# Decay attention: decays and inverse denominators kept as tokens by heads, and turned to heads by tokens

## What is computed

```
x_n   = layernorm(x) * ln1_w + ln1_b
q,k,v = x_n @ q_w + q_b, x_n @ k_w + k_b, x_n @ v_w + v_b        # (T, 128), 16 heads of 8
phi_q = elu(q) + 1 ;  phi_k = elu(k) + 1
lam   = maximum(sigmoid(x_n @ dec_w + dec_b), LAM_MIN)           # (T, 16): one decay per token and head
v_ext = concat([v, 1])                                           # nine columns per head
forward  S_t = S_(t-1) * lam_t + phi_k_t * v_t                   # scan over the tokens
backward R_t = lam_t * (phi_k_t * v_t + R_(t+1))                 # scan from the last token back
out   = phi_q . (S + R)                                          # summed over a head's 8 features
attn  = out[..., :8] / maximum(out[..., 8:], EPS)
x     = x + attn @ o_w + o_b
```

## Time and profile before

| what | us |
|---|---|
| median of 3 runs (lowest, highest) | 1849.06 (1844.62, 1851.38) |
| the profiled execution | 1840.17 |
| its span, first to last instruction | 1838.4 |
| first block of decay attention | 1371 to 1428 |
| second block of decay attention | 1428 to 1592 |

### The profile page before, as it was taken

How to read it: one execution, slowest core, us unless ns; L and a number is a source line. 1 busy time by engine, 2 the same in 40 slices (tenths; PEclk the granted TensorE clock), 3 DMA queues, 4 the chain that set the end, 5 groups by cost and what they waited for, 6 DMA issues and landing times. The chain is left out here.

```text
span 1838.4 us, 21584 instructions
## 1 busy us (share of the span) xinstructions
PE 1607.5 (87%) x7285; PEld 675.5 (37%) x7285; DVE 1352.3 (74%) x1951; ACT 856.2 (47%) x1493; POOL 222.4 (12%) x145
## 2 busy tenths in 40 slices
PE   6987589999999999999998799899984446589999
PEld 3433212222222222222223344466651112266665
DVE  5775798888888888888851777556666999745554
ACT  2443417777777777777776434322223000132221
POOL 2222300000000000000000122211100334201110
PEclk8998659999999999999999999899996767799999
DMA  6000310011001100120000000000000000000000
GB/s 171 4 0 1 124 30 8 15 28 37 12 15 28 33 15 15 28 32 10 2 2 1 1 0 0 1 1 0 0 1 0 0 1 0 1 1 6 6 6 7
DMA packets 32017, 29.42 MB, mean 16 GB/s; under 512 B 7789, under 2 KB 27033, under 8 KB 31929
## 3 DMA queue, kind: packets, MB, share of 16 engines
q1 hardware_dynamic: 31928, 28.31, 6.1%
HBM read 22.13 MB, written 4.19 MB: 14 GB/s over the span
## 5 line engine op out<-in xcount | busy, mean ns | idle before, releaser
L1350 DVE TENSOR_REDUCE mx<-ps 128x1 f32<-128x1024 f32 x512 | 603.1, 1219 | 108.9 <-PE ps L1262 107.6
L1338 ACT ACTIVATE xT<-ps 128x512 f32<-128x512 f32 x512 | 277.8, 598 | 123.4 <-PE ps L1285 117.0
L1262 PE MATMUL ps<-k,q 72*128 72x512 bf16 x1024 | 324.0, 399 | 11.0 <-DVE mx L1350 9.3
L1285 PE MATMUL ps<-q,k 84*128 84x512 bf16 x1024 | 311.7, 383 | 8.9 <-ACT xT L1338 6.4
L1338 ACT ACTIVATE xn<-ps 128x512 f32<-128x512 f32 x512 | 278.1, 601 | 83.9 <-PE ps L1285 79.1
L1285 PEld LDWEIGHTS ps<-q,k 84*128 84x128 bf16 x1024 | 96.4, 97 | 372.7 <-ACT xn L1338 152.6
L854 ACT ACTIVATE silu<-ps 128x512 f32<-128x512 f32 x144 | 85.3, 596 | 265.2 <-PE ps L827 261.8
L889 DVE TENSOR_TENSOR hid<-ps,silu 128x512 f32<-128x512 f32 x144 | 97.8, 689 | 90.2 <-PE ps L831 88.5
L827 PE MATMUL ps<-xT,ew 128*128 (+1 forms) x288 | 150.4, 604 | 6.4 <-PEq L1718 4.8
L817 PEld LDWEIGHTS ps<-ew,hid 128*128 128x128 f32 x1152 | 138.7, 192 | 30.6 <-issue 29.9
L831 PE MATMUL ps<-xT,ew 128*128 (+1 forms) x288 | 148.8, 599 | 0.0
(11 more groups left out here) (239 smaller groups left out, 1686.2 us busy)
## 6 DMA issues: line engine op xcount, KB each, us to landing
k<-k_parts SPq DMA_DIRECT2D x90, 64.0 KB
q<-q_parts SPq DMA_DIRECT2D x144, 32.0 KB
k<-k_parts SPq DMA_DIRECT2D x108, 32.0 KB
ew<-in_L_ffn_w_dram SPq DMA_DIRECT2D x2, 1024.0 KB
wraw<-in_L_ffn_w_dram SPq DMA_DIRECT2D x3, 512.0 KB, 6.7
q_parts<-part SPq DMA_DIRECT2D x4, 384.0 KB, 3.9
k_parts<-part SPq DMA_DIRECT2D x4, 384.0 KB, 2.6
v<-values SPq DMA_DIRECT2D x8, 144.0 KB, 6.1
```

The source lines that it names most:

```text
L1262: mm = nc.tensor.matmul(m.ps[:, S1B[2 * (i % 2) + kc % 2], :], queries, k1[:, h, kc * CHUNK:(kc + 1) * CHUNK], start=True, stop=True)
L1285: nc.tensor.matmul(m.ps[:, S2B[n % len(S2B)], :], k2[:, h, kt * P:(kt + 1) * P], q[:, qc, h, :], start=True, stop=True).then_inc(s2_ready, 1)
L1338: nc.scalar.activation(ex[kt % P_RING][:, h, :], m.ps[:, S2B[n % len(S2B)], :], ACT.Exp)\
L1350: nc.vector.reduce_max(mx[:, h, qt, kc:kc + 1], m.ps[:, 2 * (i % 2):2 * (i % 2) + 2, :], AX.XY)\
```

## The change

First block. The decay job of 128x512 on PE becomes four small matmuls with the tokens stationary and dec_w (128x16) moving, so that tokens lie on the partitions and 16 heads along them; the results go to bank 3 or 5. DVE adds the bias (`decay_logits`, 128x64), ACT takes exp(-z) of 128x64, and DVE adds 1 and takes the reciprocal of 128x64; then one tensor_scalar takes the maximum and writes each value eight times (128x512, `lamc`). PE multiplies that with the identity (`spread_decays`, bank 4), which turns it to heads by tokens, and ACT copies the bank to lam (`store_decays`). Banks for q and k are now three, n % 3, and each waits for job n - 3.

Second block. The denominators come from 16 small matmuls (qs stationary, one column of each head of same_head moving, 128x16 each). DVE clips and inverts 128x256. ACT, which now has a list, writes each value eight times (128x2048, into attT), PE turns it with 16 matmuls against the identity into banks 0 to 3, and ACT copies the four banks to inv. All of that stands in PE's list in front of the first `pick` product.

```diff
@@ first block, PE @@
+                def spread_decays(c):
+                    pe.wait_ge(lamc_ready, c + 1)
+                    if c >= 1:
+                        pe.wait_ge(lam_ready, c)
+                    for j in range(TPC):
+                        last = nc.tensor.matmul(m.ps[:, 4, j * P:(j + 1) * P],
+                                                lamc[:, c % 2, j, :], m.ident[:, :], start=True, stop=True)
+                    last.then_inc(spread, 1)
...
+                    if s == 1:
+                        if c >= 2:
+                            pe.wait_ge(zdec_ready, c - 1)
+                        for t in range(c * TPC, (c + 1) * TPC):
+                            last = nc.tensor.matmul(m.ps[:, DB[c % 2], t * H:(t + 1) * H], m.xT[:, t * P:(t + 1) * P], m.dec_w[:, :],
+                                                    start=True, stop=True)
+                        last.then_inc(zdec_turned, 1)
+                        if c >= 1:
+                            spread_decays(c - 1)
+                spread_decays(CHUNKS - 1)
@@ first block, ACT: features(c) and what follows it @@
-                            nc.scalar.activation(elow[:, n % 2, :], m.ps[:, n % 4, :], ACT.Exp, bias=m.neg_dec_b[:, 0:1],
-                                                 scale=-1.0).then_inc(exped, 1)
+                    act.wait_ge(zdec_ready, c + 1)
+                    nc.scalar.activation(edec[:, t, :], zdec[:, t, :], ACT.Exp, scale=-1.0).then_inc(edec_ready, 1)
+                def store_decays(c):
+                    act.wait_ge(spread, c + 1)
+                    nc.scalar.activation(lam[:, c * CHUNK:(c + 1) * CHUNK], m.ps[:, 4, :], ACT.Copy).then_inc(lam_ready, 1)
...
                     features(c)
+                    if c >= 1:
+                        store_decays(c - 1)
+                store_decays(CHUNKS - 1)
@@ first block, DVE @@
-                        step(nc.vector.tensor_scalar(one_plus[:, :], elow[:, n % 2, :], 1.0, None, ALU.add))
-                        step(nc.vector.reciprocal(sig[:, :], one_plus[:, :]))
-                        nc.vector.tensor_scalar(lam[:, t], sig[:, :], LAM_MIN, None, ALU.max).then_inc(feat_ready, 1)
+                def decays(c):
+                    t = slice(c * TPC, (c + 1) * TPC)
+                    dve.wait_ge(edec_ready, c + 1)
+                    step(nc.vector.tensor_scalar(one_plus[:, t, :], edec[:, t, :], 1.0, None, ALU.add))
+                    step(nc.vector.reciprocal(sig[:, t, :], one_plus[:, t, :]))
+                    if c >= 2:
+                        dve.wait_ge(spread, c - 1)
+                    nc.vector.tensor_scalar(lamc[:, c % 2, :, :].rearrange("p t (h k) -> p t h k", k=HD),
+                                            sig[:, t, :].unsqueeze(3).to_broadcast([P, TPC, H, HD]), LAM_MIN, None,
+                                            ALU.max).then_inc(lamc_ready, 1)
-                for s, c in [(s, c) for c in range(CHUNKS) for s in range(3)][2:]:
-                    feature(s, c)
+                decays(0)
+                for c in range(1, CHUNKS):
+                    feature(0, c)
+                    feature(1, c)
+                    decay_logits(c)
+                    decays(c)
@@ second block, PE @@
+                    if v == 0:
+                        pe.wait_ge(invr_ready, 1)
+                        for c in range(CHUNKS):
+                            for j in range(TPC):
+                                last = nc.tensor.matmul(m.ps[:, c, j * P:(j + 1) * P],
+                                                        attT[:, (c * TPC + j) * P:(c * TPC + j + 1) * P], m.ident[:, :],
+                                                        start=True, stop=True)
+                            last.then_inc(inv_spread, 1)
@@ second block, DVE and ACT @@
-                        nc.vector.reciprocal(inv[:, :], den[:, :]).then_inc(inv_ready, 1)
+                        nc.vector.reciprocal(invc[:, :, :].rearrange("p t h -> p (t h)"), den[:, :]).then_inc(invc_ready, 1)
...
+                act.wait_ge(invc_ready, 1)
+                nc.scalar.activation(attT[:, :].rearrange("p (t h k) -> p t h k", h=H, k=HD),
+                                     invc[:, :, :].unsqueeze(3).to_broadcast([P, TILES, H, HD]), ACT.Copy).then_inc(invr_ready, 1)
+                for c in range(CHUNKS):
+                    act.wait_ge(inv_spread, c + 1)
+                    nc.scalar.activation(inv[:, c * CHUNK:(c + 1) * CHUNK], m.ps[:, c, :], ACT.Copy).then_inc(inv_ready, 1)
```

More of the change, by code:

```diff
@@ L1527, in features @@
                 def features(c):
-                    for s in range(3):
-                        n = 3 * c + s
+                    for s in range(2):
+                        n = 2 * c + s
                         act.wait_ge(proj, n + 1)
@@ L1532, in features @@
                             act.wait_ge(feat_ready, n - 1)
[L1533 to L1538, removed]
[L1539 to L1542 removed]
+                        nc.scalar.activation(z[:, n % 2, :], m.ps[:, n % 3, :], ACT.Identity,
+                                             bias=m.qk1_bias[:, s:s + 1]).then_inc(z_ready, 1)
+                        act.wait_ge(clipped, n + 1)
+                        nc.scalar.activation(elow[:, n % 2, :], low[:, n % 2, :], ACT.Exp).then_inc(exped, 1)
+                    t = slice(c * TPC, (c + 1) * TPC)
[4 more added lines that the diff above has]
+                    nc.scalar.activation(lam[:, c * CHUNK:(c + 1) * CHUNK], m.ps[:, 4, :], ACT.Copy).then_inc(lam_ready, 1)
                 outer_norm.squares(act, CHUNKS - 1)
@@ L1574, in feature @@
-                    dve.wait_ge(feat_ready, n + 1)
+                    dve.wait_ge(z_ready, n + 1)
+                    nc.vector.tensor_scalar(low[:, n % 2, :], z[:, n % 2, :], 0.0, None, ALU.min).then_inc(clipped, 1)
+                    dve.wait_ge(exped, n + 1)
+                    nc.vector.scalar_tensor_tensor(out=phi[:, s, t], in0=z[:, n % 2, :], scalar=0.0,
+                                                   in1=elow[:, n % 2, :], op0=ALU.max, op1=ALU.add)\
+                        .then_inc(feat_ready, 1)
@@ L1640, in _ @@
                     pe.wait_ge(qs_ready, n + 1)
-                    if n == 1:
-                        pe.wait_ge(den_read, 1)
-                    for c in range(CHUNKS):
[L1644 to L1649, removed]
+                    if v == HD:
+                        for t in range(TILES):
+                            last = nc.tensor.matmul(m.ps[:, 0, t * H:(t + 1) * H], qs[:, n % 2, t * P:(t + 1) * P],
+                                                    m.same_head[:, :].rearrange("p (h k) -> p h k", k=HD)[:, :, 0],
+                                                    start=True, stop=True)
+                        last.then_inc(summed, 1)
+                        continue
+                    if v == 0:
[4 more added lines that the diff above has]
+                                                        attT[:, (c * TPC + j) * P:(c * TPC + j + 1) * P], m.ident[:, :],
+                                                        start=True, stop=True)
+                            last.then_inc(inv_spread, 1)
+                    for c in range(CHUNKS):
+                        if v == 0:
+                            pe.wait_ge(inv_ready, c + 1)
+                        last = nc.tensor.matmul(m.ps[:, c, :], m.pick[:, v, :], qs[:, n % 2, c * CHUNK:(c + 1) * CHUNK],
+                                                start=(v == 0), stop=(v == HD - 1))
                     last.then_inc(summed, 1)
```

41 lines of the change are left out of this document (27 added, 14 removed).

## The result

| | before | changed |
|---|---|---|
| median of 5 runs, us | 1845.27 | 1828.99 |
| lowest, highest | 1841.06, 1851.38 | 1826.44, 1834.38 |
| ratio | | 0.9908, 95% interval 0.9879 to 0.9936 |
| the profiled execution | 1840.17 | 1829.61 |
| its span | 1838.4 | 1827.9 |

The changed kernel is 0.9% faster, 16.3 us between the medians. The two profiled executions lie only 10.5 us apart, so the spans can't be compared as a whole. I divide each profile at three instructions that both have: DVE's first one of decay attention (the reduction to v_bias), its first of the second block (the memset of bwd), and its first of the feed-forward (the first total_norm reduction).

The account below looks back on a forecast made before the run. DVE was taken to bound both decay attention blocks. Savings of 3.3 us in the first and 12.96 in the second, less a 0.3 stall, gave 16.0 us: from the median 1849.06 to 1833.1 us, range 1826 to 1842.

Parts of the forecast that it names:

- DVE bounds both blocks: Decay attention: DVE busy 41.1 of 57 us in the first block, 155.0 of 164 in the second, so its savings shorten them.
- the handover: First block, chunk 0 to 1: the spread stands before PE's turning, so DVE goes on 1.9 us later than before.
- the tail: End of first block: PE's pieces, their result and ACT's copy come behind DVE's last decay, 2.4 us in all.
- The price of the short operations: First block, new decay part of a chunk: bias, exponential, plus one, reciprocal, widening maximum and gaps sum to 1.81 us.
- The saving of a chunk: First block, decay part on DVE: 1.81 us instead of 4.31, so each chunk saves 2.50.
- POOL's cover: Second block, round 3: the forward scan still starts 0.45 us behind POOL's addition; otherwise 1.56 us would be lost.
- The stall of 0.3 at column 3: Second block: DVE waits for PE's values of column 3, losing about 0.3 us.
- The first rival: Second block: PE's clock stays low when turning the denominators; gain 10.1 or 7.8 us, about 1839 us; chance 0.14.
- the case that had 0.85: Whole kernel: faster by more than the 0.5%, 9.2 us, that a measurement can tell from no change; chance 0.85.
- The second: Rival: handover, tail and longer PE list cost twice the estimate, overlap lost; gain under 9 us, 1842 us; chance 0.10.
- The slower one: Rival, last stages: PE's granted clock falls; over 0.5% slower from 25 us of half-speed matmul work, 1859 us; chance 0.03.
- The fourth: Rival, both blocks: the change doesn't shorten the reciprocals because their time goes with something else than length; given no chance.

Follow-up runs that it names:

- the doubled turnings: Changed kernel with each of the 16 turning matmuls of the denominators issued twice, same output; second block 152.66 us, 1.44 more than the changed kernel; one run, 1828.67 us.

## Why the prediction was right, point by point

**DVE bounds both blocks.** Right. Everything DVE lost in the second block, the block lost; in the first block what it didn't pass on is the handover, the tail and 0.32 us a chunk of waiting for ACT's exponential of the decays, all worked out ahead.

**The price of the short operations.** Right to 0.01 us: the bias 0.22 to 0.23, the exponential 0.26, plus one 0.19 to 0.20, the reciprocals 0.55 and 1.75, clip 0.41. The open one was the widening maximum, 0.43 by the row of the same operation or 0.69 by a row with a repeated operand. It took 0.43. The Trainium skill, "Vector Engine (DVE) Microarchitecture Reference", section 5.1, has such a repeated read keep two elements a cycle; the trace agrees (0.43, as without repetition), here with an element read eight times where the page's case has thirty-two. The pessimistic row was a two-input operation and did not carry over.

**The saving of a chunk.** 2.60 where I said 2.50. The step that was off by 0.1 is the gap I put behind the maximum: the next clip, which needs nothing of the maximum's result, starts 0.34 us behind the start of a maximum of 0.43.

**The handover.** DVE idle 4.41 against 4.4 forecast, by the mechanism named. The start of chunk 1 was 1.40 us later than before, counted from the block's first instruction, not 1.9: the 0.2 for the small matmuls in chunk 0 was 0.0 in this profile (the turning at 0.63 us follows on at once, as at 1391.36 in the earlier trace rows) and 0.73 in four others, where the clock rose later; the bound I had given was 1.1. That it was 0.0 in the profile compared here is luck. What remains is 0.24 of DVE's gaps (from phi's end to the decays 2.01 us, 2.25 counted: an operation that doesn't wait for the one before it follows closer) and the bias reduction at the block's start, which I had counted apart.

**The tail.** 2.47 us from DVE's last decay to ACT's end, 2.4 forecast, with bounds of 1.8 and 2.8. In the profiles that keep this tail it was 2.27 to 2.77, with 1.58 to 2.08 us of spread in it.

**The second block.** 13.08 against 12.66. POOL's cover held with 0.33 us to spare, where 0.45 was worked out. The stall of 0.3 at column 3 didn't come, and my own times didn't hold it either: by them the last bank of values is there at 1489.4, and kv, starting at 1487.6 with a piece every 0.67, wants it at 1489.6. Besides, the 32 turning pieces took 5.87 us, not 6.6, since the clock rose sooner than I took from the pick bursts (0.50 to 1482.5, 1.00 from 1482.9 on). That PE was near the path is what the doubled turnings show. The first rival, a clock that stays low, would have cost 5.9 us; none of that came.

**The sum.** The first block gave 4.07 against 3.3: 0.4 at the handover (the bias reduction left aside), 0.1 in each of two chunks and 0.2 at the end, where the next block's memset came 0.33 us behind ACT's copy, but 0.57 behind DVE's last lam before. The second gave 0.4 more than forecast, 0.3 of it the stall. Together that is 17.15 in the profile against 16.0 forecast; the medians give 16.3. The median itself came out at 1829.0, 4.1 below the 1833.1 I forecast, of which 3.8 is that the runs of before had a median of 1845.27 and not 1849.06 once there were five of them. The nine microseconds between the profiled execution and the median that I noted are most likely scatter of what lies ahead of decay attention; the runs that make the median have no profile, so this is inferred. In all ten profiles its start lies between 1371.54 and 1378.86 with no pattern by edit, while A of one code is reproduced to 0.6 us, B to 0.05, and what lies behind to 1.8. Between the profiles of before and after, 2.6 of the 6.6 us came in the first stage, where the granted clock was 0.89 and 0.92 in the stretches that lengthened (0.94 and 0.96 before), and 4.0 around the transfers ahead of softmax attention (ACT waits 14.2 us there, before 10.2). Why these differ from one execution to the next was not tried.

**The rivals.** The interval of the change, 0.6 to 1.2%, is clear of 0.5%, so it is the case that had 0.85. The first rival's low clock didn't come: over the two blocks the granted clock was 0.68 and 0.77, before 0.65 and 0.74. The second asked for a gain under 9 us. The slower one asked for a fall of the clock in the last stages: it is 1.00 there, and everything behind decay attention took 246.01 us against 245.94. The fourth, that a reciprocal doesn't follow its length, falls with 0.55 and 1.75 us.

## What to carry to other kernels

A value that is the same for eight partitions is cheaper to work out once per value with tokens on the partitions, if its engine is the bound: the reciprocals, at 6.25 ns an element, had an eighth of the elements and fell from 3.35 to 0.55 and from 12.95 to 1.75 us, and the turning back cost PE and ACT work that they had room for. The price is in the order: every step that a saving hands to another engine stands in that engine's list in front of something, so ask for each what is queued behind it (here the turning of the next chunk, and behind that z) and move what doesn't depend on it ahead; here that and one moved addition gave 8.1 us on top of the 17.2 of the change. And look who stands still beside whom: POOL's addition beside the first scan cost the scan 4.3 us, and nothing where DVE waited for PE.

## What the runs showed of the hardware that I had not expected

Chunk 0's wait has a short and a long case, 3.34 to 3.39 and 4.11 to 4.12 us, by whether PE's clock rises from 0.50 before or after its turning of the third chunk; it was the long one in half of the eight profiles with the small decay matmuls. Eight pieces of small fp32 matmuls took 0.96 us with 16 moving columns and 1.16 with 128 at the higher clock, 1.73 and 2.08 at the lower, so an eighth of the columns saved PE only a sixth of the time here.
